# A two-layer attention and mixture-of-experts kernel: the products with the swapped rows of the rotation go from GpSimd to VectorE, from the fourth step on

## The chip, the cores and the metric

One core of one Trainium2 chip. The metric is the device time of one execution in microseconds (us). Names of engines in the rows: PE is TensorE's matmul, PEld its weight load, DVE is VectorE, ACT is ScalarE, POOL is GpSimd, SP is SyncE.

## The reference, cut to what matters

The input is 16 sequences of 256 tokens with 128 features. Two layers follow one another, each of them an attention and a feed-forward part that read the same normalised input and are added to it:

```python
xn = _layernorm(x)
x = x + L0_attn(xn) + L0_ffn(xn)      # windowed attention, 8 heads of 64; 8 experts of width 256 and a shared one
xn = _layernorm(x)
x = x + L1_attn(xn) + L1_ffn(xn)      # gated attention; 32 experts of width 64 and a shared one
```

The change touches the rotation of queries and keys in the attention of layer 0. The same projection `qk` serves as query and as key, with two tables each:

```python
bq = bq * jnp.cos(qf) * qs    + _rotate_half(bq) * jnp.sin(qf) * qs
bk = bk * jnp.cos(freqs) * inv_s + _rotate_half(bk) * jnp.sin(freqs) * inv_s
```

So for each of q and k there are two products (the rows with the cosine table, the swapped rows with the signed sine table) and one sum.

## The kernel before, in words

**Tiling and steps.** A step handles 2 sequences, 512 tokens; there are 8 steps, numbered 0 to 7. Features lie on the 128 partitions, tokens along the row, so most operands are tiles of 128x512 in float32. The 8 heads of layer 0 are handled as 4 pairs `p` (a pair fills 128 partitions), the 9 experts of layer 0 as `e` = 8 (the shared one) and 0 to 7.

**Stages.**
**The experts of layer 0.** For each expert TensorE makes two halves of the hidden layer (`up0_half`, lines 449 to 451), ScalarE applies Gelu (L1033), then the weight of the expert for each token is multiplied in: the half `c` = 0 on VectorE (`hidden`, L1405), the half `c` = 1 on GpSimd (`hidden`, L1773), both from the tile `pw` and the weights `wb` in SBUF. TensorE sums the results (`down0`, L586), for the half `c` only after that engine's event:

```python
w.wait_ge(*(HID_POOL if c else HID_DVE).at(s, e))
```

TensorE's order in `experts0` is: shared expert down; then `up0(1)`, `down0(0)`, `project(n, 0)`, `up0(2)`, `down0(1)`, `project(n, 1)`, `up0(3)`, `down0(2)`, `project(n, 2)`, `up0(4)`, `down0(3)`, `project(n, 3)`, `values(n, 0)`, `up0(5)`, `down0(4)`, `values(n, 1)`, `values(n, 2)`, `up0(6)`, `down0(5)`, `values(n, 3)`, `up0(7)`, `down0(6)`, `attention_out` (L594), `down0(7)`, with n = s + 1.

**PSUM banks.** `project(n, 0)` and `project(n, 2)` write bank 2, `project(n, 1)` and `project(n, 3)` bank 6 (L473); `values(n, 1)` writes bank 2 after `project(n, 2)` (L480). A bank that held a projection is free again at the event `STRAIGHT` of that pair, which the second product from PSUM counts up:

```python
freed[k] = STRAIGHT.at(s, p)
```

**The rotation of a pair**, before the change. `rope_in` on VectorE swaps neighbouring rows (`stream_shuffle`, L1324, PSUM to `qks`), multiplies the projection in PSUM by the two cosine tables (L1325 to `rtmp`, L1326 to `qka`, whose end is `STRAIGHT`). `rope_turn` on GpSimd multiplies the swapped rows by the two sine tables (L1759 to `kr`, L1761 to `qr`; both operands in SBUF). `rope_add` on VectorE adds (L1333, L1335; both operands in SBUF). The buffers `qks`, `rtmp` and `qka` have two slots, so `rope_in` of pair p waits for `rope_add` of pair p - 2. VectorE's order in `experts0` is `hidden` 0, 1, 2, `rope_in` 0, `hidden` 3, `rope_in` 1, `hidden` 4, `rope_add` 0, `rope_in` 2, `hidden` 5, `rope_add` 1, `rope_in` 3, `hidden` 6, `rope_add` 2, `hidden` 7, `rope_add` 3. GpSimd's is `hidden` 0, 1, `normalise` 0, 1 (L1767, the attention's division, once the denominators have come by DMA), `hidden` 2, `rope_turn` 0, `hidden` 3, `rope_turn` 1, `hidden` 4, `normalise` 2, 3, `hidden` 5, `rope_turn` 2, `hidden` 6, `rope_turn` 3, `hidden` 7.

Of the kernel before, what the change touches and what calls it, by code (L numbers as in the profile page):

```python
# [10 lines left out]
ALU = mybir.AluOpType  # L11
# [74 lines left out]
def two_layers(nc, A, out):  # L86
    pe, act, dve, pool, sp = nc.tensor, nc.scalar, nc.vector, nc.gpsimd, nc.sync
    with ExitStack() as ctx:
        def sb(name, shape, dt=F32):
            return ctx.enter_context(nc.sbuf_tensor(name, shape, dt))  # L90
# [4 lines left out]
        def event(name, per_step=1, unit=1):  # L95
            return Event(semaphore(name), per_step, unit)
# [4 lines left out]
        def weight(name, shape, src=None, dt=F32):  # L101
            t = sb("w_" + name, shape, dt)
            weights[name] = (t, A[name] if src is None else src)
            return t
# [5 lines left out]
        rope0 = weight("rope0", [P, 4, SEQ])  # L110
# [54 lines left out]
        qks = sb("qks", [P, 2, TOK])  # L165
        rtmp = sb("rtmp", [P, 2, TOK])
        qr = sb("qr", [P, PAIRS, TOK])
        kr = sb("kr", [P, PAIRS, TOK])
# [58 lines left out]
        def bank(k):  # L227
            return ps[:, k, :]
# [8 lines left out]
        def columns(s):  # L237
# [20 lines left out]
        PROJECTED, SWAPPED, STRAIGHT, TURNED_K, TURNED_Q, ROPED = (event(n, PAIRS) for n in (  # L258
            "projected", "swapped", "straight", "turned_k", "turned_q", "roped"))
        VALUES, VALUE_ROWS = event("values", TILES), event("value_rows", TILES)  # L260
        SCORES, MAXIMA, EXPS, INVERTED, WEIGHED, OUT_COLS = (event(n, UNITS) for n in (
            "scores", "maxima", "exps", "inverted", "weighed", "out_cols"))
# [36 lines left out]
        def spread(ap, dims):  # L299
            return bass.AP(tensor=ap.tensor, offset=ap.offset, ap=[list(ap.ap[0])] + [list(d) for d in dims])  # L300

        def seqs(ap):
            return ap.rearrange("p (g t) -> p g t", g=G)

        def table(rope, i):
            return spread(rope[:, i, :], [(0, G), (1, SEQ)])
# [968 lines left out]
        def dve_program():  # L1275
            w = Waits(dve)
# [42 lines left out]
            def rope_in(s, p, k):  # L1319
                h = p % 2  # L1320
                w.wait_ge(LOADED["rope0"], 16)
                w.wait_ge(*PROJECTED.at(s, p))
                w.wait_ge(*(ROPED.at(s, p - 2) if p >= 2 else KV1.at(s - 2)))
                dve.stream_shuffle(qks[:, h, :], bank(k), PAIR_SWAP).then_inc(*SWAPPED.one)  # L1324
                dve.tensor_tensor(seqs(rtmp[:, h, :]), seqs(bank(k)), table(rope0, 0), ALU.mult)  # L1325
                dve.tensor_tensor(seqs(qka[:, h, :]), seqs(bank(k)), table(rope0, 2),  # L1326
                                  ALU.mult).then_inc(*STRAIGHT.one)

            def rope_add(s, p):
                h = p % 2  # L1330
                w.wait_ge(*STRAIGHT.at(s, p))
                w.wait_ge(*TURNED_K.at(s, p))
                dve.tensor_tensor(kr[:, p, :], kr[:, p, :], rtmp[:, h, :], ALU.add)  # L1333
                w.wait_ge(*TURNED_Q.at(s, p))
                dve.tensor_tensor(qr[:, p, :], qr[:, p, :], qka[:, h, :], ALU.add).then_inc(*ROPED.one)  # L1335
# [193 lines left out]
            def attention(s):  # L1529
                first, second = s == 0, s == 1  # L1530
                if first:
                    maxima(s, 0)
                    maxima(s, 1)
                    rope_add(s, 1)
                    rope_in(s, 3, 1)
# [47 lines left out]
            def experts0(s):  # L1583
# [4 lines left out]
                if more:  # L1588
                    rope_in(n, 0, 2)
                hidden(s, 3)  # L1590
                if more:
                    rope_in(n, 1, 6)
# [136 lines left out]
        def pool_program():  # L1729
            w = Waits(pool)  # L1730
# [23 lines left out]
            def rope_turn(s, p):  # L1754
                h = p % 2
                w.wait_ge(LOADED["rope0"], 16)
                w.wait_ge(*SWAPPED.at(s, p))
                w.wait_ge(*SCORES.at(s - 1))
                pool.tensor_tensor(seqs(kr[:, p, :]), seqs(qks[:, h, :]), table(rope0, 1),  # L1759
                                   ALU.mult).then_inc(*TURNED_K.one)  # L1760
                pool.tensor_tensor(seqs(qr[:, p, :]), seqs(qks[:, h, :]), table(rope0, 3),  # L1761
                                   ALU.mult).then_inc(*TURNED_Q.one)

            def normalise(s, p):
                w.wait_ge(*DEN_WIDE.at(s))
                w.wait_ge(*OUT_COLS.at(s))
                pool.tensor_tensor(atc[:, p, :], atc[:, p, :], wide[:, p, :], ALU.mult).then_inc(*NORMALISED.one)  # L1767

            def hidden(s, e):
                n = 2 * place0(e) + 1  # L1770
                w.wait_ge(*GELU.at(s, n))
                w.wait_ge(*wb_layer0(e // 2, s))
                pool.tensor_tensor(hid[:, n % 4, :], hid[:, n % 4, :], wb[:, e, :],  # L1773
                                   ALU.mult).then_inc(*HID_POOL.one)
# [61 lines left out]
            def experts0(s):  # L1836
                n, more = s + 1, s < LAST
                for e in range(E0):
                    hidden(s, e)
                    if more and e in (2, 3, 5, 6):  # L1840
                        rope_turn(n, (0, 0, 0, 1, 0, 2, 3)[e])
                    if e in (1, 4):
                        normalise(s, 2 * (e // 4))
                        normalise(s, 2 * (e // 4) + 1)
# [44 lines left out]
            for s in range(STEPS):  # L1889
                attention(s)  # L1890
                if s == 1:
                    experts0_and_chain1(s)
                else:
                    experts0(s)
                if s:
                    experts1(s)
# [5 lines left out]
        act_program()  # L1902
        pool_program()
        dve_program()
        pe_program()

# [98 lines left out]
```

## Time and profile before

| what | value |
|---|---|
| three runs, median (lowest to highest) | 1113.2 us (1112.49 to 1113.9) |
| profiled execution: its own time | 1117.62 us |
| profiled execution: span from first to last instruction | 1116.3 us |
| mean granted clock of TensorE | 0.978 of full |
| PE busy | 1033.4 us (93%) |
| DVE busy | 713.6 us (64%) |
| ACT busy | 517.7 us (46%) |
| POOL busy | 472.3 us (42%) |
| time of one of the steps 3 to 6 | 131.5 us |

How to read it: a busy share is an average over stages that have different limits. The step's time is the distance between the starts of the same instruction in neighbouring steps, 467.11 us in step 3 and 598.58 us in step 4 for the down products of expert 3 (L586).

### The profile page before, as it was taken

How to read it: one execution, taken by the hardware profiler on the slowest of the kernel's cores; microseconds unless marked ns; L12 is line 12 of the kernel's file. 1: busy time of each engine (PE TensorE's matmuls, PEld its weight loads, DVE VectorE, ACT ScalarE, POOL GpSimd, SP SyncE). 2: the span in 40 equal slices, each digit the busy share in tenths (PEclk: the TensorE clock that was granted, in tenths of full speed). 3: DMA queues.
4: the chain of work that ended last, by engine and by line, in shares of the span. 5: the costliest groups of instructions: out<-in, count | busy, mean ns of one | idle time of the engine just before them, and what ended most of it. 6: DMA issues, size and time to landing. Idle time of an engine off the chain costs nothing.

```text
span 1116.3 us, 13293 instructions
## 1 busy us (share of the span) xinstructions
PE 1033.4 (93%) x4472; PEld 627.5 (56%) x4472; DVE 713.6 (64%) x1469; ACT 517.7 (46%) x1208; POOL 472.3 (42%) x353
## 2 busy tenths in 40 slices
PE   4799886899999989999899998999989998989988
PEld 2454554366555666556565565546655565655655
DVE  4658765748748487575857488484884758622833
ACT  3453672162554536444374525636265453634222
POOL 4747334434137521664208441285314741053433
PEclk9899997799999999999999999999999999989999
DMA  6040140060042302322023210422004120242051
GB/s 248 30 133 1 30 114 1 0 144 20 11 136 57 85 0 86 80 66 57 10 89 86 66 39 10 129 62 76 12 24 137 51 67 1 87 97 72 24 125 47
DMA packets 34581, 72.77 MB, mean 65 GB/s; under 512 B 4553, under 2 KB 5330, under 8 KB 34130
## 3 DMA queue, kind: packets, MB, share of 16 engines
q1 hardware_dynamic: 33074, 68.59, 22.1%
q10 hardware_dynamic: 1440, 3.35, 0.8%
q8 instruction: 35, 0.57, 0.2%
q14 instruction: 32, 0.26, 0.1%
HBM read 69.04 MB, written 2.88 MB: 64 GB/s over the span
## 4 chain that ended last, share of the span: by engine, by line
PE 70%; DVE 10%; issue 3%; POOL 3%; ACT 2%; DVEq 0%; POOLq 0%; ACTq 0%
PE ps L586 9%; PE ps L698 9%; PE ps L449 7%; PE ps L450 7%; PE ps L451 7%; PE ps L521 5%; PE ps L497 4%; PE ps L509 4%; PE ps L673 3%; PE ps L594 2%; PE ps L473 2%; PE ps L480 2%; PE ps L644 2%; PE ps L662 1%; PE ps L652 1%
## 5 line engine op out<-in xcount | busy, mean ns | idle before, releaser
L1773 POOL TENSOR_TENSOR pw<-pw,wb 128x512 f32<-128x512 f32 x64 | 94.1, 1471 | 204.9 <-ACT pw L1033 204.9
L1111 ACT ACTIVATE wide<-ps 128x512 f32<-128x512 f32 x136 | 81.0, 596 | 177.2 <-PE ps L451 176.4
L586 PE MATMUL ps<-pw,w_w 128*128 128x512 f32 x288 | 147.0, 627 | 16.9 <-DVE pw L1405 10.8
L1780 POOL TENSOR_TENSOR atc<-atc,wide 128x512 f32<-128x512 f32 x64 | 82.4, 1288 | 169.4 <-DVE atc L1520 169.4
L1033 ACT ACTIVATE pw<-ps,w_cols 128x512 f32<-128x512 f32 x144 | 98.5, 687 | 86.5 <-PE ps L451 83.5
L1405 DVE TENSOR_TENSOR pw<-pw,wb 128x512 f32<-128x512 f32 x64 | 61.8, 966 | 100.7 <-ACT pw L1033 100.6
L992 ACT ACTIVATE pw<-ps,nmax 128x256 f32<-128x256 f32 x256 | 117.3, 475 | 6.8 <-DVE nmax L1341 6.7
L1350 DVE COPY pt<-ps 128x512 f32<-128x512 f32 x128 | 82.3, 685 | 30.8 <-PE ps L509 30.8
L1341 DVE TENSOR_REDUCE nmax<-ps 128x4 f32<-128x1024 f32 x64 | 78.2, 1223 | 36.3 <-PE ps L497 35.8
L586 PEld LDWEIGHTS ps<-pw,w_w 128*128 128x128 f32 x288 | 52.9, 195 | 71.8 <-issue 26.2
L1780 POOL TENSOR_TENSOR pt<-pt,wide 128x512 f32<-128x512 f32 x48 | 61.5, 1281 | 67.3 <-DVE pt L1520 66.2
L449 PE MATMUL ps<-y1c,eg 128*128 128x512 f32 x112 | 84.8, 757 | 0.0
L449 PE MATMUL ps<-y0c,w 128*128 128x512 f32 x144 | 80.2, 557 | 1.2 <-ACT pt L1087 1.2
L521 PE MATMUL ps<-pt,vr 128*64 128x256 f32 x512 | 71.4, 401 | 8.0 <-DVE pt L1350 7.8
L1520 DVE TENSOR_TENSOR pt<-ps,wb 128x512 f32<-128x512 f32 x64 | 44.2, 691 | 49.0 <-PE ps L451 47.6
L509 PE MATMUL ps<-ident,pw 128*128 128x128 f32 x512 | 70.1, 280 | 5.8 <-ACT pw L992 3.6
L698 PE MATMUL ps<-pt,w_ed 128*128 128x512 f32 x128 | 66.6, 604 | 9.5 <-DVE pt L1524 9.5
L497 PE MATMUL ps<-kr,qr 64*128 64x256 f32 x512 | 74.5, 410 | 0.4 <-DVE qr L1335 0.4
L1520 DVE TENSOR_TENSOR atc<-ps,wb 128x512 f32<-128x512 f32 x64 | 44.1, 691 | 46.1 <-PE ps L451 39.5
L509 PEld LDWEIGHTS ps<-ident,pw 128*128 128x128 f32 x512 | 56.3, 142 | 25.2 <-issue 18.2
L698 PE MATMUL ps<-atc,w_ed 128*128 128x512 f32 x128 | 67.4, 608 | 0.0
L1751 POOL TENSOR_TENSOR rstd<-ve,half_power 128x8 f32<-128x8 f32 x16 | 28.5, 1783 | 88.2 <-DVE ve L1291 88.2
(223 smaller groups left out, 2188.2 us busy)
## 6 DMA issues: line engine op xcount, KB each, us to landing
wb<-scratch SPq DMA_DIRECT2D x128, 256.0 KB, 4.0
wb<-scratch SPq DMA_DIRECT2D x32, 512.0 KB, 5.7
wide<-scratch SPq DMA_DIRECT2D x16, 512.0 KB, 6.0
xin<-in_x SPq DMA_DIRECT2D x8, 256.0 KB, 2.9
out<-wide SPq DMA_DIRECT2D x8, 256.0 KB, 2.1
w_w<-in_w ACTq DMA_DIRECT2D x1, 1152.0 KB, 11.4
wb<-in_w SPq DMA_DIRECT2D x1, 1152.0 KB, 11.6
w_ed<-in_ed ACTq DMA_DIRECT2D x1, 1024.0 KB, 17.1
```

The source lines that it names most:

```text
L449: pe.matmul(bank(k), high, moving[:, 0, :], start=True, stop=False)
L497: m = pe.matmul(ps[:, b + par, qt * SEQ:(qt + 1) * SEQ], qr[rows, p, q0:q0 + P], kr[rows, p, g * SEQ:(g + 1) * SEQ], start=False, stop=Tru ...
L509: m = pe.transpose(bank(6 + par)[:, j * P:(j + 1) * P], pw[:, u % 2, 2 * par + qt, kt * P:(kt + 1) * P], ident[:, :])
L521: m = pe.matmul(bank(b)[64 * par:64 * par + 64, 0:SEQ], vr[:, 2 * g + kt, 2 * p + par, :], pt[:, u % 2, 4 * par + 2 * kt:4 * par + 2 * kt ...
L586: pe.matmul(bank(ACC), w2[:, e, c, :], hid[:, n % 4, :], start=n == 0, stop=n == 2 * E0 + 1).then_inc(*DOWN0.one)
L698: pe.matmul(bank(ACC), sd[:, :] if c < 0 else ed[:, c, :], hh[(c + 1) % len(hh)], start=c < 0, stop=c == CH1 - 1).then_inc(*DOWN.one)
L992: m = act.activation(pw[:, u % 2, j, :], ps[:, b + j // 2, (j % 2) * SEQ:(j % 2 + 1) * SEQ], ACT.Exp, bias=nmax[:, u % 3, j:j + 1], scale= ...
L1033: act.activation(hid[:, n % 4, :], bank(UPS[n % 4]), ACT.Gelu, bias=cols[:, C_B1 + 2 * e + c:C_B1 + 2 * e + c + 1], scale=1.0).then_inc(*G ...
L1350: dve.tensor_copy(pt[:, u % 2, 4 * par:4 * par + 4, :].rearrange("p a q -> p (a q)"), bank(6 + par)).then_inc(*PT.one)
L1520: dve.tensor_tensor(hh[h], bank(k), wb[:, c % (2 * RING), :], ALU.mult).then_inc(*HH_WEIGHED.one)
L1773: pool.tensor_tensor(hid[:, n % 4, :], hid[:, n % 4, :], wb[:, e, :], ALU.mult).then_inc(*HID_POOL.one)
L1780: pool.tensor_tensor(hh[h], hh[h], sgl[:, (c + 1) % 3, :], ALU.mult).then_inc(*HH_POOL.one)
```

## The change

From the fourth step on (step 3; it is prepared during step 2), `rope_in` on VectorE also makes the two products with the swapped rows, right behind its two products from PSUM, and GpSimd's program leaves `rope_turn` out. Steps 0, 1 and 2 are rotated as before: GpSimd's `rope_turn` for step 1 is in `experts0(0)`, for step 2 in `experts0_and_chain1(1)`. What is computed is the same.

```diff
--- before.py
+++ after.py
@@ -1325,6 +1325,13 @@
                 dve.tensor_tensor(seqs(rtmp[:, h, :]), seqs(bank(k)), table(rope0, 0), ALU.mult)
                 dve.tensor_tensor(seqs(qka[:, h, :]), seqs(bank(k)), table(rope0, 2),
                                   ALU.mult).then_inc(*STRAIGHT.one)
+                if s > 2:
+                    w.wait_ge(*SWAPPED.at(s, p))
+                    w.wait_ge(*SCORES.at(s - 1))
+                    dve.tensor_tensor(seqs(kr[:, p, :]), seqs(qks[:, h, :]), table(rope0, 1),
+                                      ALU.mult).then_inc(*TURNED_K.one)
+                    dve.tensor_tensor(seqs(qr[:, p, :]), seqs(qks[:, h, :]), table(rope0, 3),
+                                      ALU.mult).then_inc(*TURNED_Q.one)
 
             def rope_add(s, p):
                 h = p % 2
@@ -1837,7 +1844,7 @@
                 n, more = s + 1, s < LAST
                 for e in range(E0):
                     hidden(s, e)
-                    if more and e in (2, 3, 5, 6):
+                    if s < 2 and e in (2, 3, 5, 6):
                         rope_turn(n, (0, 0, 0, 1, 0, 2, 3)[e])
                     if e in (1, 4):
                         normalise(s, 2 * (e // 4))
```

On VectorE, in the middle of `experts0` of a step from 2 to 6, from the product of expert 3 on; first as it was (L1405 is `hidden`, L1324 to L1326 `rope_in`, L1333 and L1335 `rope_add`):

```order
L1405 TENSOR_TENSOR pw<-pw,wb 128x512
L1324 STREAM_SHUFFLE qks<-ps 128x512
L1325 TENSOR_TENSOR rtmp<-ps,w_rope 128x512
L1326 TENSOR_TENSOR qka<-ps,w_rope 128x512
L1405 TENSOR_TENSOR pw<-pw,wb 128x512
L1333 TENSOR_TENSOR kr<-kr,rtmp 128x512
L1335 TENSOR_TENSOR qr<-qr,qka 128x512
L1324 STREAM_SHUFFLE qks<-ps 128x512
L1325 TENSOR_TENSOR rtmp<-ps,w_rope 128x512
L1326 TENSOR_TENSOR qka<-ps,w_rope 128x512
```

The same place in the changed program, where `hidden` is L1412, the new products are L1331 and L1333, and the sums L1340 and L1342:

```order
L1412 TENSOR_TENSOR pw<-pw,wb 128x512
L1324 STREAM_SHUFFLE qks<-ps 128x512
L1325 TENSOR_TENSOR rtmp<-ps,w_rope 128x512
L1326 TENSOR_TENSOR qka<-ps,w_rope 128x512
L1331 TENSOR_TENSOR kr<-qks,w_rope 128x512
L1333 TENSOR_TENSOR qr<-qks,w_rope 128x512
L1412 TENSOR_TENSOR pw<-pw,wb 128x512
L1340 TENSOR_TENSOR kr<-kr,rtmp 128x512
L1342 TENSOR_TENSOR qr<-qr,qka 128x512
L1324 STREAM_SHUFFLE qks<-ps 128x512
L1325 TENSOR_TENSOR rtmp<-ps,w_rope 128x512
L1326 TENSOR_TENSOR qka<-ps,w_rope 128x512
```

The last row of both is the instruction that frees bank 2 for `values(n, 1)`. Between it and the projection of pair 0 there are four more instructions than before (those of pairs 0 and 1).

On GpSimd, in the same stage, as it was (L1773 is `hidden`, L1759 and L1761 `rope_turn`, L1767 `normalise`):

```order
L1773 TENSOR_TENSOR pw<-pw,wb 128x512
L1759 TENSOR_TENSOR kr<-qks,w_rope 128x512
L1761 TENSOR_TENSOR qr<-qks,w_rope 128x512
L1773 TENSOR_TENSOR pw<-pw,wb 128x512
L1759 TENSOR_TENSOR kr<-qks,w_rope 128x512
L1761 TENSOR_TENSOR qr<-qks,w_rope 128x512
L1773 TENSOR_TENSOR pw<-pw,wb 128x512
L1767 TENSOR_TENSOR atc<-atc,wide 128x512 x2
```

The whole of GpSimd's stage in the changed program, where `hidden` is L1780 and `normalise` L1774:

```order
L1780 TENSOR_TENSOR pw<-pw,wb 128x512 x2
L1774 TENSOR_TENSOR atc<-atc,wide 128x512 x2
L1780 TENSOR_TENSOR pw<-pw,wb 128x512 x3
L1774 TENSOR_TENSOR atc<-atc,wide 128x512 x2
L1780 TENSOR_TENSOR pw<-pw,wb 128x512 x3
```

Eight of its twenty instructions are gone, and nothing is left between the products of experts 2, 3 and 4. TensorE's and ScalarE's instructions are the same and in the same order.

## Rows read from the trace of the kernel before

**Rows 1.** The profile page: busy time of three engines, and the granted clock in slices.
```profile
PE 1033.4 (93%) x4472; PEld 627.5 (56%) x4472; DVE 713.6 (64%) x1469; ACT 517.7 (46%) x1208; POOL 472.3 (42%) x353
...
PEclk9899997799999999999999999999999999989999
```

**Rows 2.** Chain of waits, window 445 to 496 us: start, length, engine, output, line.
```profile
467.11 1.78 PE ps L586 x4
...
472.03 1.90 PE ps L586 x4
473.93 1.77 PE ps L480 x4
...
481.07 0.94 PE ps L586 x2
...
482.01 1.13 PE ps L586 x2
```

**Rows 3.** VectorE in order of time, window 440 to 500 us.
```profile
459.85 0.73 DVE L1324 STREAM_SHUFFLE qks<-ps 128x512 f32<-128x512 f32 x1
...
463.20 0.88 DVE L1405 TENSOR_TENSOR pw<-pw,wb 128x512 f32<-128x512 f32 x1 [1.45 <-ACT pw L1033]
...
467.17 1.08 DVE L1405 TENSOR_TENSOR pw<-pw,wb 128x512 f32<-128x512 f32 x1 [1.25 <-ACT pw L1033]
468.18 1.75 DVE L1333 TENSOR_TENSOR kr<-kr,rtmp 128x512 f32<-128x512 f32 x1
469.85 1.76 DVE L1335 TENSOR_TENSOR qr<-qr,qka 128x512 f32<-128x512 f32 x1
...
472.97 0.69 DVE L1326 TENSOR_TENSOR qka<-ps,w_rope 128x512 f32<-128x512 f32 x1
...
484.11 1.75 DVE L1405 TENSOR_TENSOR pw<-pw,wb 128x512 f32<-128x512 f32 x1
...
487.46 0.68 DVE L1335 TENSOR_TENSOR qr<-qr,qka 128x512 f32<-128x512 f32 x1
492.21 0.69 DVE L1515 TENSOR_TENSOR atc<-ps,wide 128x512 f32<-128x512 f32 x1 [4.08 <-ACT wide L1111]
```

**Rows 4.** GpSimd in order of time, same window.
```profile
459.69 2.62 POOL L1767 TENSOR_TENSOR atc<-atc,wide 128x512 f32<-128x512 f32 x2 [2.41 <-DMA wide<-scratch]
462.26 1.28 POOL L1773 TENSOR_TENSOR pw<-pw,wb 128x512 f32<-128x512 f32 x1
...
465.19 1.28 POOL L1761 TENSOR_TENSOR qr<-qks,w_rope 128x512 f32<-128x512 f32 x1
...
471.03 1.73 POOL L1773 TENSOR_TENSOR pw<-pw,wb 128x512 f32<-128x512 f32 x1
472.72 2.94 POOL L1767 TENSOR_TENSOR atc<-atc,wide 128x512 f32<-128x512 f32 x2
...
480.24 1.72 POOL L1773 TENSOR_TENSOR pw<-pw,wb 128x512 f32<-128x512 f32 x1
```

**Rows 5.** Waits by engine and line, window 445 to 490 us: total, times, longest.
```profile
PEld ps L480 <- DVE qka L1326: 0.6, 1, 0.6
```

**Rows 6.** Windows, step 7: length, busy PE, PEld, DVE, ACT, POOL, PEclk, DMA, GB/s.
```profile
985.40:988.80 3.40, 1.07 (x3) 0.20 (x2) 1.36 (x1) 0.92 (x2) 3.40 (x3) 1.00 0.61 145
988.80:992.20 3.40, 2.77 (x5) 1.55 (x6) 0.00 (x0) 0.00 (x0) 1.80 (x2) 0.50 0.08 20
992.20:995.60 3.40, 3.40 (x8) 1.98 (x7) 0.69 (x1) 1.37 (x2) 0.74 (x1) 0.50 0.56 146
```

**Rows 7.** The same view: inside step 0, and the end of step 3.
```profile
115.00:118.40 3.40, 0.99 (x7) 0.76 (x8) 3.19 (x10) 1.92 (x10) 0.00 (x0) 1.00 0.00 0
118.40:121.80 3.40, 3.40 (x17) 1.91 (x17) 2.72 (x12) 0.00 (x0) 2.12 (x2) 0.50 0.24 77
121.80:125.20 3.40, 3.40 (x30) 2.27 (x28) 2.96 (x6) 2.21 (x9) 3.18 (x4) 1.00 0.21 61
545.00:548.40 3.40, 1.99 (x7) 0.94 (x6) 3.16 (x7) 2.90 (x7) 0.00 (x0) 1.00 0.00 0
```

## The prediction

> **What bounds the kernel now.** The page comes first. TensorE is busy for 93% of the span, and its granted clock stands at 9 tenths or more through all of the middle [rows 1]. So time is won or lost where TensorE is made to stop, and the question for this change is whether VectorE or GpSimd makes it stop in the stage `experts0` of steps 2 to 6, where rotations for steps 3 to 7 are made. Steps 3 to 6 repeat to 0.1 us, so I read step 3 for all five.
>
> The chain of waits through that stage is TensorE from one end to the other [rows 2]. Its small stops can be read there: four matmul passes of `down0` in a row take 1.72 us when nothing is late (two take 0.86), so `down0(3)` with 1.78 has lost 0.06, `down0(4)` with 1.90 has lost 0.18, and `down0(6)`, 0.94 and 1.13 with 0.01 between, has lost 0.36 us. Together 0.6 us a step. The last, at 482.01, is GpSimd's product of expert 6, which ran from 480.24 to 481.96 [rows 4]: that half is late because a pair's sine products stand ahead of it on GpSimd.
>
> VectorE in order of time [rows 3] is the view that decides. Up to 467 it has gaps, 1.45 us ahead of `hidden` 3 and 1.25 ahead of `hidden` 4. From 467.17 to 488.1 it has none. The instruction that frees bank 2, L1326 of pair 2, starts at 472.97 and ends at 473.66; TensorE begins the values that need this bank at 473.93 [rows 2], and its weight load had waited for just that instruction [rows 5]. The margin there is 0.27 us.
>
> **What two engines do to each other.** A VectorE product of two SBUF tiles takes 0.68 us at 487.46, when GpSimd is idle, and 1.75 us at 468.18, when GpSimd works [rows 3]. A GpSimd product takes 1.28 us at 462.26 and 1.73 us at 471.03 [rows 4]. Instructions that read PSUM and one SBUF tile are not slowed: L1326 takes 0.69 us while GpSimd runs [rows 3, 4]. So where both want SBUF pairs they alternate: the VectorE product is held 1.07 us, the GpSimd product 0.45 us. Of the 0.68 us, 0.07 overlap with the next instruction (468.18 plus 1.75 against 469.85), so from start to start it is 0.61 free and 1.68 held. The Trainium skill, in "SBUF — State Buffer", section "Who interferes with whom", has the rule: the interface that both share is locked, and the second to come is blocked until the first has finished its whole instruction. That GpSimd's side waits only 0.45 us behind a product of 0.68 us is less than this rule gives; at the rule's 0.68 each alternation below would be about 0.23 us longer, seven of them 1.6 us a step, and the time about 8 us above my sum. The rows decide, so 0.45 stands.
>
> **The change, part by part.** It removes 8 of GpSimd's 20 products per step from 2 to 6 (40 in all) and adds 8 of two SBUF tiles to VectorE (40 in all), with no DMA and no other move. The waits added on VectorE (`SWAPPED`, `SCORES`) are for events long past: the shuffle is two instructions back. I take them at nothing; if they cost 0.1 us each, that is up to 0.4 us a step ahead of the bank.
>
> Free of any hold the 8 products are 8 x 0.61 = 4.9 us. Four of them, 2.4 us, lie ahead of the instruction that frees bank 2, and the two gaps of 2.7 us could just take them. What decides is the holding. The gaps were also the times at which VectorE stood out of GpSimd's way. I lay out VectorE after the shuffle of pair 0, which starts at 459.85 as before:
> - shuffle and two products from PSUM, 1.85 us, to 461.7.
> - first sine product: GpSimd is in its second `normalise` until 462.3 (459.69 plus 2.62 [rows 4]), held 0.5, to 462.8.
> - second sine product: held by GpSimd's `hidden` 2, 1.68, to 464.5.
> - `hidden` 3, ready since 463.2 [rows 3], held by GpSimd's `hidden` 3, 1.68, to 466.2.
> - pair 1: 1.85 to 468.0, then a free sine product (GpSimd waits for Gelu) to 468.6, then one held by `hidden` 4 to 470.3.
> - `hidden` 4, held by `normalise` 2, to 472.0; the first sum of pair 0, held by `normalise` 3, to 473.7; the second, held by `hidden` 5, to 475.4.
> - pair 2: a short wait for the sum, 0.1, then 1.85 us: bank 2 is free at 477.3.
>
> That is 5.6 us from PSUM, 8 products at 0.61, and 6.9 us held, where before it was 5.6, 4 products, 2.7 idle and 2.7 held. TensorE starts the values at 477.35 in place of 473.93, 3.4 us late. A weight load that could not be made ahead costs 0.27 more, as the 1.13 in place of 0.86 at 482.01 shows [rows 2]. That is 3.7 us a step. `hidden` 3 and 4 also end within 0.3 us of when TensorE asks, but that lateness lies inside the wait for bank 2.
>
> Behind it GpSimd has run dry and VectorE works unheld: the rest of pair 2, `hidden` 5, two sums, pair 3 and `hidden` 6 end near 484.7, just when TensorE comes (481.07 plus 3.7). So of the 0.36 us at `down0(6)` 0.27 stay. The last sum ends at 488.9, and VectorE's next work comes only at 492.21 plus the delay, behind 4.08 us of idle time [rows 3], so nothing of the delay is won back, and nothing is added. GpSimd gains 8 x 1.28 us or more of idle time for which nobody waits.
>
> **The clock.** A stop of 3.3 us has a second price. In step 7 TensorE was busy for 1.07 of 3.40 us, and then its clock was at half, the 1.2 GHz level, for 6.8 us [rows 6]; in step 0, 0.99 of 3.40 was followed by 3.4 us at half and then full clock [rows 7]; 1.99 busy of 3.40 at the end of step 3 left it at full [rows 7]. My stop is nearer the first two. Half clock for 3.4 us of work costs 1.7 us, less the 0.27 at `hidden` 6, which is then in time: 1.4 us a step. With 6.8 us at half, part of it inside the stop, it is about 2.6. I take the shorter one, since TensorE has work without a break behind this stop, as in step 0, while in step 7 it was interrupted again.
>
> **The sum:** 3.7 + 1.4 = 5.1 us a step, five steps, 25.5 us. The profiled execution took 1117.62 us, 4.4 above the median of 1113.2; against the median the forecast is 1138.7 us. Bounds of the unknown: no holding at all would give back the 0.6 us of small stops, 3.0 us faster; the clock at half twice as long in each step, 31.5 us slower.
>
> **The rivals.**
> - **Faster, 1110.2 us.** GpSimd with 12 products in place of 20 is out of the way, VectorE's sine products slip into the gaps, and the 0.6 us of stops per step go. For it: the free time of the new products, 2.4 us, fits into 2.7 us of gaps, and GpSimd's expert 6 is no longer late. It holds as long as bank 2 is free by 473.9, which leaves 14.05 - 5.6 - 4.9 = 3.5 us for holding. Against it: I count 6.9 us, seven meetings, and only three may happen. Chance 0.06.
> - **No change or little**, between 1111 and 1120 us, if about half the meetings happen. 0.06, of it 0.04 within 0.2%.
> - **The stop without the clock**: 5 x 3.7 = 18.5, 1131.7 us. For it: where the stop falls in time is open, and TensorE works right before and after. 0.20.
> - **The clock at half for 6.8 us each time**: 5 x 6.3 = 31.5, 1144.7 us. For it, rows 6. 0.23.
> - The forecast itself: 0.45. That the change doesn't do what it says is ruled out by the order of the instructions.
>
> **How the numbers follow.** The range takes in the three slower cases but for the edges: 1125 to 1149 us, the upper end with 0.5 us more a step if the added waits or a longer hold cost something. About 0.15 lies outside. A measurement of this kernel tells 0.2%, about 2.2 us, from no change. Faster by more 0.06, within 0.04, slower 0.90.
>
> **What would show it.** In the changed profile: L1331 and L1333 with a mean near 1.2 us, most of them 0.68 or 1.75; VectorE without a gap from 459.9 to bank 2; a wait of PE's L480 for DVE's L1326 of about 3.3 us, five times; GpSimd idle ahead of `hidden` 6; PEclk low right behind that wait. The forecast is wrong if L480 is not late, if TensorE's first late instruction is a `down0` that waits for `hidden`, or if the clock stays full in all five.

## The result, and the profile after

The changed kernel takes 1134.19 us (median of 4 runs, 1132.8 to 1136.67) against 1113.55 us of the kernel before beside it (4 runs, 1112.49 to 1115.12). The ratio is 1.0187 with an interval of 1.0163 to 1.021: slower by 20.6 us. The forecast was 1138.7 us, 25.5 us slower, in a range of 1125 to 1149.

Busy time and granted clock on the page of the changed kernel, which answer to [rows 1]:

```profile
PE 1035.6 (91%) x4472; PEld 629.2 (55%) x4472; DVE 732.4 (65%) x1509; ACT 517.2 (46%) x1208; POOL 414.8 (37%) x313
...
PEclk9799899899999999999999999999999999999999
```

TensorE's busy time and clock are nearly those of before. The span is 19.1 us longer (1135.4 against 1116.3) and TensorE is busy for 2.2 us more, so most of the added time, about 17 us, lies in stops of TensorE and not in its work.

**Where it lies.** ScalarE loads its table for Gelu at the start of the stage (L1033) and its table for SiLU at the end (L1111), so the distance of the two loads is the length of the stage `experts0` in which the rotation is made. In order of time on ScalarE in step 3, before:

```profile
445.17 1.28 ACT L1033 ACT_TABLE_LOAD   x1
...
490.19 1.28 ACT L1111 ACT_TABLE_LOAD   x1
```

and after:

```profile
447.58 1.28 ACT L1033 ACT_TABLE_LOAD   x1
...
497.57 1.28 ACT L1111 ACT_TABLE_LOAD   x1
```

That is 45.0 us before and 50.0 us after. In steps 2, 3, 4, 5 and 6 the same distance is 49.98, 49.99, 49.97, 49.98 and 48.58 us after the change, and 44.99 to 45.02 before: 23.4 us in all. Between these stages nothing grew: steps 2 to 5 have 86.4 us outside the stage in both profiles, step 6 has 86.0. Elsewhere the changed kernel's profiled execution was the shorter one: by 2.6 us ahead of step 2 (granted clock 0.95 there against 0.94, TensorE busy for 1.7 us less), and by 1.6 us in the stage of step 7 (42.40 us at a clock of 0.92 before, 40.82 us at 0.96 after). 23.4 - 2.6 - 1.6 is 19.2 us, the difference of the spans to 0.1 us.

**The stop.** Waits of TensorE over the whole execution, total, times and longest:

```profile
PE ps L480 <- DVE qka L1326: 17.0, 5, 3.4
```

This is the values' matmul waiting for the instruction that frees bank 2, five times 3.4 us. VectorE in order of time, step 3 (everything is 2.41 us later than before, as the two table loads of L1033 show):

```profile
462.27 0.73 DVE L1324 STREAM_SHUFFLE qks<-ps 128x512 f32<-128x512 f32 x1
...
464.10 1.18 DVE L1331 TENSOR_TENSOR kr<-qks,w_rope 128x512 f32<-128x512 f32 x1
465.20 1.76 DVE L1333 TENSOR_TENSOR qr<-qks,w_rope 128x512 f32<-128x512 f32 x1
466.88 1.75 DVE L1412 TENSOR_TENSOR pw<-pw,wb 128x512 f32<-128x512 f32 x1
...
470.38 0.68 DVE L1331 TENSOR_TENSOR kr<-qks,w_rope 128x512 f32<-128x512 f32 x1
470.98 1.75 DVE L1333 TENSOR_TENSOR qr<-qks,w_rope 128x512 f32<-128x512 f32 x1
...
474.34 1.76 DVE L1340 TENSOR_TENSOR kr<-kr,rtmp 128x512 f32<-128x512 f32 x1
476.02 1.75 DVE L1342 TENSOR_TENSOR qr<-qr,qka 128x512 f32<-128x512 f32 x1
...
479.12 0.68 DVE L1326 TENSOR_TENSOR qka<-ps,w_rope 128x512 f32<-128x512 f32 x1
...
485.95 1.75 DVE L1412 TENSOR_TENSOR pw<-pw,wb 128x512 f32<-128x512 f32 x1
...
499.59 0.69 DVE L1522 TENSOR_TENSOR atc<-ps,wide 128x512 f32<-128x512 f32 x1 [7.76 <-ACT wide L1111]
```

GpSimd beside it:

```profile
461.80 2.93 POOL L1774 TENSOR_TENSOR atc<-atc,wide 128x512 f32<-128x512 f32 x2 [2.11 <-DMA wide<-scratch]
464.68 3.39 POOL L1780 TENSOR_TENSOR pw<-pw,wb 128x512 f32<-128x512 f32 x2
470.65 1.53 POOL L1780 TENSOR_TENSOR pw<-pw,wb 128x512 f32<-128x512 f32 x1 [2.57 <-ACT pw L1033]
472.14 3.41 POOL L1774 TENSOR_TENSOR atc<-atc,wide 128x512 f32<-128x512 f32 x2
475.51 1.71 POOL L1780 TENSOR_TENSOR pw<-pw,wb 128x512 f32<-128x512 f32 x1
485.65 1.51 POOL L1780 TENSOR_TENSOR pw<-pw,wb 128x512 f32<-128x512 f32 x1 [8.43 <-ACT pw L1033]
```

The reader is to see three things. First, from 462.27 on VectorE has no gap but 0.1 us ahead of the shuffle of pair 2; the two that stood in [rows 3] are filled. Second, of the eight two-tile products up to the sum at 476.02, six take 1.75 or 1.76 us, the first 1.18, and one, at 470.38, is free with 0.68. Third, GpSimd's rows lie exactly beside the held ones: the second of its divisions from 461.80 holds the first product, its two `hidden` from 464.68 the next two, `hidden` at 470.65 one, the two divisions from 472.14 two, and `hidden` at 475.51 the last. Then GpSimd is idle until 485.65; VectorE is held again at 485.95. Bank 2 is free at 479.80, on the clock of before 477.4, where it was 473.7.

The end of the delay is in the same view: 7.76 us of idle time on VectorE ahead of L1522 in place of 4.08 [rows 3].

All 20 of the second sine products of a pair (shortest, median, longest in ns):

```profile
L1333 DVE TENSOR_TENSOR qr<-qks,w_rope x20: 678/1218/1757, 328.8 to 895.0; 128x512 f32<-128x512 f32 x20
```

**The clock.** Windows of step 3 around the stop (length, busy PE, PEld, DVE, ACT, POOL, granted clock), and then the same of step 6:

```profile
477.70:481.10 3.40, 1.25 (x3) 0.73 (x4) 3.28 (x8) 0.09 (x1) 0.00 (x0) 0.97 0.00 0
481.10:484.50 3.40, 3.40 (x8) 1.99 (x7) 3.28 (x7) 1.66 (x3) 0.00 (x0) 0.53 0.43 112
```

```profile
883.90:887.30 3.40, 1.76 (x4) 0.45 (x3) 3.28 (x4) 0.69 (x2) 2.52 (x2) 1.00 0.00 0
887.30:890.70 3.40, 1.65 (x5) 0.87 (x5) 3.40 (x6) 0.49 (x1) 0.00 (x0) 1.00 0.00 0
```

In step 3 the clock was at half, the 1.2 GHz level, for 3.4 us from about 481 on, a good 1 us after TensorE had begun again; so it was in steps 2, 4 and 5. In step 6 the same stop of 3.4 us had no low stretch at all: the clock stayed at full through it and behind it. That is the difference between 49.98 and 48.58 us: the low stretch costs 1.4 us, and without it the change costs 3.56 us a step. Why step 6 escaped the rows don't show. The busy times in the two pairs of lines differ only because the lines are laid differently over the stop: a line from 886.90 to 890.30, which lies over the stop of step 6 as the first lies over that of step 3, has the same 1.25 us busy, at full clock. The Trainium skill, "TensorE: Matmul & The Clock Gate", section "Why this matters for your kernels", warns of idle gaps between bursts of matmuls as what brings the clock down; four of the five stops agree, and the fifth, as long as they, does not.

### The profile page after: what moved, and what is told of

It reads as the page before. It is cut to its first block, busy times and chain, and to the rows that moved or that the text cites. A ratio compares the mean times of both kernels' runs of the same rounds, so it can differ in the third digit from the quotient of the medians.

```text
span 1135.4 us, 13288 instructions
## 1 busy us (share of the span) xinstructions
PE 1035.6 (91%) x4472; PEld 629.2 (55%) x4472; DVE 732.4 (65%) x1509; ACT 517.2 (46%) x1208; POOL 414.8 (37%) x313
## 4 chain that ended last, share of the span: by engine, by line
PE 61%; DVE 16%; issue 4%; POOL 3%; ACT 3%; DVEq 0%; POOLq 0%; ACTq 0%
PE ps L698 9%; PE ps L449 6%; PE ps L450 6%; PE ps L451 6%; PE ps L586 5%; PE ps L521 5%; PE ps L497 4%; PE ps L509 4%; PE ps L673 2%; PE ps L594 2%; DVE pw L1412 2%; PE ps L644 2%; PE ps L480 2%; DVE qr L1333 1%; PE ps L652 1%
## 5 line engine op out<-in xcount | busy, mean ns | idle before, releaser
L1780 POOL TENSOR_TENSOR pw<-pw,wb 128x512 f32<-128x512 f32 x64 | 95.2, 1492 | 265.4 <-ACT pw L1033 265.4
L1111 ACT ACTIVATE wide<-ps 128x512 f32<-128x512 f32 x136 | 80.9, 595 | 177.1 <-PE ps L451 176.3
L586 PE MATMUL ps<-pw,w_w 128*128 128x512 f32 x288 | 144.5, 620 | 16.9 <-DVE pw L1412 10.9
L1033 ACT ACTIVATE pw<-ps,w_cols 128x512 f32<-128x512 f32 x144 | 98.4, 687 | 87.4 <-PE ps L451 84.9
L1412 DVE TENSOR_TENSOR pw<-pw,wb 128x512 f32<-128x512 f32 x64 | 66.1, 1033 | 86.2 <-ACT pw L1033 86.2
L449 PE MATMUL ps<-y0c,w 128*128 128x512 f32 x144 | 83.1, 577 | 1.2 <-ACT pt L1087 1.2
```

Of the source, the lines that this page charges most:

```text
L449: pe.matmul(bank(k), high, moving[:, 0, :], start=True, stop=False)
L586: pe.matmul(bank(ACC), w2[:, e, c, :], hid[:, n % 4, :], start=n == 0, stop=n == 2 * E0 + 1).then_inc(*DOWN0.one)
L1033: act.activation(hid[:, n % 4, :], bank(UPS[n % 4]), ACT.Gelu, bias=cols[:, C_B1 + 2 * e + c:C_B1 + 2 * e + c + 1], scale=1.0).then_inc(*G ...
L1412: dve.tensor_tensor(hid[:, n % 4, :], hid[:, n % 4, :], wb[:, e, :], ALU.mult).then_inc(*HID_DVE.one)
```

## The experiments

Theory H, from the prediction: the delay comes of the places where VectorE's two-tile products meet GpSimd's, and of what stands ahead of the release of bank 2. Theory W, its rival: VectorE has simply been given more work than the stage has room for. In the diffs `n` is the step prepared. Lengths of the stage are read as above, from ScalarE's two table loads; clock times of a run are brought to the clock of before by the table load of L1033 in step 3, at 445.17 us there. The medians of before beside these runs are 1114.07 us for the first four (18 runs) and 1113.58 us for the others (18 runs).

### GpSimd's divisions later, VectorE untouched

```diff
-                    if e in (1, 4):
+                    if 1 < s < LAST and e == 5:
+                        for p in range(PAIRS):
+                            normalise(s, p)
+                    if not 1 < s < LAST and e in (1, 4):
                         normalise(s, 2 * (e // 4))
                         normalise(s, 2 * (e // 4) + 1)
```

> The changed kernel with VectorE untouched; in steps 2 to 6 GpSimd makes its four divisions (normalise) after the product of expert 5 in place of two after expert 1 and two after expert 4. Theory H (the delay is made of holding: VectorE's two-tile products meet GpSimd's): bank 2 is free at about 472.2 on the clock of the kernel before, 5 us earlier than in the change, so the wait of TensorE's L480 for VectorE's L1326 (3.4 us, five times) is gone. The meetings come later instead, around expert 6, whose product on VectorE ends near 484.7: a stop of about 3.7 us in front of down0(6) takes its place. Time about as the change, 1131 to 1145 us, with another stop. Theory W (the delay is only VectorE's added work, 8 products more whatever GpSimd does): the wait of L480 stays at 3.4 us, five times, and nothing stops at down0(6).

Measured: 1139.16 us (2 runs), ratio 1.0219, 1.0182 to 1.0256. The wait of 3.4 us at L480 is gone from all steps. TensorE's wait in the stage of step 3 (total, times, longest), VectorE in order of time, and GpSimd:

```profile
PE ps L586 <- DVE pw L1412: 4.0, 1, 4.0
```

```profile
474.89 0.69 DVE L1326 TENSOR_TENSOR qka<-ps,w_rope 128x512 f32<-128x512 f32 x1
...
486.35 1.74 DVE L1412 TENSOR_TENSOR pw<-pw,wb 128x512 f32<-128x512 f32 x1
```

```profile
477.87 6.34 POOL L1774 TENSOR_TENSOR atc<-atc,wide 128x512 f32<-128x512 f32 x4
```

Bank 2 is free at 475.58, which is 472.2 on the clock of before (3.39 us less), as laid out. The four divisions from 477.87 on, which end at 484.21, now hold two sums and part of a sine product ahead of `hidden` 6; the next sine product and `hidden` 6 itself are held by GpSimd's products of experts 6 and 7, which had waited behind the divisions. `hidden` 6 ends at 488.09, 484.7 on that clock, and TensorE stops 4.0 us for it. GpSimd's own product of expert 6 has become late by this edit as well, but it ends about 2 us sooner. The stage takes 50.1 to 50.3 us. So the same VectorE program misses another deadline when GpSimd's program alone is changed. W expected the wait at L480 to stay: it falls.

### What the change gives: GpSimd relieved, and nothing else

```diff
-                    if more and e in (2, 3, 5, 6):
+                    if s < 2 and e in (2, 3, 5, 6):
                         rope_turn(n, (0, 0, 0, 1, 0, 2, 3)[e])
...
-                w.wait_ge(*TURNED_K.at(s, p))
+                if s < 3:
+                    w.wait_ge(*TURNED_K.at(s, p))
```

(and the same for `TURNED_Q`, on the kernel before)

> The kernel before, with the 40 products with the swapped rows left out on both engines from step 3 on (so queries and keys of steps 3 to 7 keep old values in place of these terms). It takes from the change only what it gives: GpSimd's relief. Theory H: hidden 3, 4 and 6 are no longer late, 0.5 to 0.6 us a step, 2.5 to 3 us in all: 1110 to 1111 us against 1113.5. Rival R (GpSimd's relief frees more than the small stops, since earlier events let DMAs and the next stage start earlier): 5 us or more, below 1108.5 us.

Measured: 1111.75 us (10 runs), ratio 0.9967, 0.9946 to 0.9987. The stage takes 44.38 to 44.41 us in all five steps, 0.6 us less than before. The chain of waits in it shows where, against 1.78, 1.90 and 0.94 plus 1.13 in [rows 2]:

```profile
465.82 1.72 PE ps L586 x4
...
470.65 1.72 PE ps L586 x4
...
479.49 1.72 PE ps L586 x4
```

`down0(3)`, `down0(4)` and `down0(6)` all take 1.72 us, the time of four passes when nothing is late. Over the five steps that is the 3.1 us of the rival "faster" (the medians differ by 2.3), and it is all that the relief is worth.

### The same number of products, but from PSUM

```diff
+                if s > 2:
+                    w.wait_ge(*SCORES.at(s - 1))
+                    dve.tensor_tensor(seqs(kr[:, p, :]), seqs(bank(k)), table(rope0, 1),
+                                      ALU.mult).then_inc(*TURNED_K.one)
+                    dve.tensor_tensor(seqs(qr[:, p, :]), seqs(bank(k)), table(rope0, 3),
+                                      ALU.mult).then_inc(*TURNED_Q.one)
                 dve.tensor_tensor(seqs(rtmp[:, h, :]), seqs(bank(k)), table(rope0, 0), ALU.mult)
                 dve.tensor_tensor(seqs(qka[:, h, :]), seqs(bank(k)), table(rope0, 2),
                                   ALU.mult).then_inc(*STRAIGHT.one)
-                if s > 2:
-                    w.wait_ge(*SWAPPED.at(s, p))
-                    w.wait_ge(*SCORES.at(s - 1))
-                    dve.tensor_tensor(seqs(kr[:, p, :]), seqs(qks[:, h, :]), table(rope0, 1),
-                                      ALU.mult).then_inc(*TURNED_K.one)
-                    dve.tensor_tensor(seqs(qr[:, p, :]), seqs(qks[:, h, :]), table(rope0, 3),
-                                      ALU.mult).then_inc(*TURNED_Q.one)
```

> The changed kernel with the 40 products on VectorE in the same number and nearly the same place, but reading the projection in PSUM in place of the swapped rows in SBUF (so the swapped rows are not what is multiplied), and put ahead of the two straight products, so that the bank is freed after them. One SBUF tile per product, so nothing to hold. Theory H: VectorE does all the added work (about 0.6 us each) and is still in time: bank 2 is free at about 473.4, no wait at L480, and 0.5 us a step faster than before, 1110 to 1112 us. Theory W: the added work is there in full and even ahead of the bank's release, so the wait at L480 stays above 2.4 us a step (four products of 0.6 us) and the time above 1125 us.

Measured: 1109.05 us (6 runs), ratio 0.9956, 0.9937 to 0.9975. The stage takes 44.4 to 44.5 us in four steps and 44.9 in one. VectorE and GpSimd in order of time:

```profile
457.00 0.68 DVE L1327 TENSOR_TENSOR kr<-ps,w_rope 128x512 f32<-128x512 f32 x1
457.59 0.68 DVE L1329 TENSOR_TENSOR qr<-ps,w_rope 128x512 f32<-128x512 f32 x1
...
461.18 0.67 DVE L1327 TENSOR_TENSOR kr<-ps,w_rope 128x512 f32<-128x512 f32 x1
...
469.25 0.68 DVE L1332 TENSOR_TENSOR qka<-ps,w_rope 128x512 f32<-128x512 f32 x1
469.85 1.26 DVE L1411 TENSOR_TENSOR pw<-pw,wb 128x512 f32<-128x512 f32 x1
```

```profile
455.95 2.88 POOL L1773 TENSOR_TENSOR atc<-atc,wide 128x512 f32<-128x512 f32 x2 [2.16 <-DMA wide<-scratch]
...
460.48 1.27 POOL L1779 TENSOR_TENSOR pw<-pw,wb 128x512 f32<-128x512 f32 x1 [0.42 <-ACT pw L1033]
```

The products at 457.00 and 457.59 run in the middle of GpSimd's two divisions and take 0.68 us; the one at 461.18 runs beside `hidden` and takes 0.67. In the change the two products of pair 0, at the same place beside the divisions and `hidden`, took 1.18 and 1.76 us. Bank 2 is free at 469.93, 473.4 on the clock of before (3.49 us more), although all added work stands ahead of its release. This is the run that tells the theories apart: VectorE has room for 40 more products, and what it has no room for is holding.

### Two of the four products behind the release of the bank

VectorE's order in steps 2 to 6, with H for `hidden`, R for `rope_in`, M for the two sine products, A for `rope_add`:

```diff
-H0 H1 H2 R0 M0 H3 R1 M1 H4 A0 R2 M2 H5 A1 R3 M3 H6 A2 H7 A3
+H0 H1 H2 R0 M0 H3 R1 H4 A0 R2 M1 M2 H5 A1 R3 M3 H6 A2 H7 A3
```

> The changed kernel with the two sine products of pair 1 moved on VectorE from behind that pair's straight products to behind those of pair 2, so that they no longer stand ahead of the release of bank 2. Nothing else is moved. Theory H, laid out as in the prediction: bank 2 is free at about 474.0, TensorE waits there 0.3 us in place of 3.4, and then hidden 5 and hidden 6 are each late by 0.3 to 1 us: in all 1.4 us a step over the kernel before and no fall of the clock in these steps, so about 7 us slower than before, near 1120 us. Theory W: two products fewer ahead of the bank save 1.2 of the 3.4 us, so 2.2 us of wait at L480 stay, and 2.5 us a step or more, over 1126 us with the clock's part.

Measured: 1119.3 us (7 runs), ratio 1.0057, 1.0037 to 1.0077, 5.2 us slower. The stage takes 46.3 us in steps 2, 3 and 5, 1.3 over before, 46.4 in step 6 and 47.1 in step 4. VectorE in order of time, and TensorE's wait in the stage:

```profile
472.73 0.68 DVE L1326 TENSOR_TENSOR qka<-ps,w_rope 128x512 f32<-128x512 f32 x1
...
481.05 0.68 DVE L1414 TENSOR_TENSOR pw<-pw,wb 128x512 f32<-128x512 f32 x1
```

```profile
PE ps L586 <- DVE pw L1414: 0.8, 1, 0.8
```

Bank 2 is free at 473.41, 474.0 on the clock of before: 3.4 us earlier than in the change, although only two products of 0.68 us were moved. With them went two held times of 1.07 us: that of the second of the two, and that of `hidden` 4, which no longer meets GpSimd. (The first of the two had been free.) L480 does not wait to speak of. What is late now is `hidden` 6 at 481.05, for which TensorE stops 0.8 us, and the clock stays at full. The size came out as laid out (1.3 us against 1.4); of its parts, `hidden` 5 was expected late too, and no wait for it shows.

### All of it on VectorE, in an order that avoids the meetings

```diff
-H0 H1 H2 R0 M0 H3 R1 M1 H4 A0 R2 M2 H5 A1 R3 M3 H6 A2 H7 A3
+H0 H1 H2 R0 R1 M0 H3 A0 H4 R2 M1 M2 H5 A1 A2 H6 R3 M3 A3 H7
```

> The changed kernel (all 8 sine products of a step on VectorE, reading the swapped rows in SBUF), with VectorE's order in steps 2 to 6 rewritten: sine products and sums are put where GpSimd is between two of its products, and hidden 6 ahead of pair 3. Same instructions, same tiles. Theory H (the delay is a matter of where VectorE's two-tile products meet GpSimd's, and of what stands ahead of the bank): laid out by hand with 0.61 us free and 1.68 us held, TensorE never stops for VectorE or GpSimd in this stage; the stage, 45.0 us before and 50.0 in the change, is 44.4 us; five times 0.6 us faster than before, about 3 us. Theory W (VectorE simply has too much to do in this stage): some stop of TensorE for VectorE stays wherever it is put, the stage is over 46 us, the time over 1120 us.

Measured: 1109.62 us (10 runs), ratio 0.9964, 0.9951 to 0.9978. ScalarE's two table loads of step 3, and VectorE:

```profile
441.44 1.28 ACT L1033 ACT_TABLE_LOAD   x1
...
485.83 1.28 ACT L1111 ACT_TABLE_LOAD   x1
```

```profile
459.91 0.68 DVE L1333 TENSOR_TENSOR kr<-qks,w_rope 128x512 f32<-128x512 f32 x1
...
462.18 0.68 DVE L1414 TENSOR_TENSOR pw<-pw,wb 128x512 f32<-128x512 f32 x1
...
474.49 0.67 DVE L1414 TENSOR_TENSOR pw<-pw,wb 128x512 f32<-128x512 f32 x1
```

44.4 us, as in three other steps and 5.6 us less than in the change with the same instructions. Both straight parts come first, while GpSimd divides; of the products of pair 0 one is held, and then GpSimd waits for Gelu. `hidden` 6 starts at 474.49 with pair 3's work behind it, 478.2 on the clock of before. In step 4 the stage took 45.1 us; there GpSimd's divisions began 3.4 us after it was ready, waiting for the denominators' DMA, and `hidden` 2 stood behind them.

### The kernel before, in a better order

```diff
-VectorE H0 H1 H2 R0 H3 R1 H4 A0 R2 H5 A1 R3 H6 A2 H7 A3
+VectorE H0 H1 H2 R0 H3 R1 A0 H4 R2 H5 A1 H6 R3 H7 A2 A3
-GpSimd  H0 H1 N0 N1 H2 M0 H3 M1 H4 N2 N3 H5 M2 H6 M3 H7
+GpSimd  H0 H1 N0 H2 M0 H3 N1 H4 N2 M1 H5 N3 H6 M2 M3 H7
```

(N is a division, `normalise`)

> The kernel before (sine products on GpSimd), with both orders in steps 2 to 6 rewritten: GpSimd takes the product of the next expert ahead of divisions and sine products where it can, VectorE takes sums before hidden and hidden 6 and 7 earlier. If the 0.6 us a step of small stops are all that is to be had, this gives them as well as the change does in a good order: a stage of 44.4 us, about 3 us faster than before. If moving work to VectorE has a worth of its own, it falls behind g5_new_order by more than 0.2 us a step.

Measured: 1109.87 us (9 runs), ratio 0.9967, 0.9952 to 0.9981, with a stage of 44.4 us but in step 4 (45.2). This cannot be told from the run before it: where the sine products run is worth nothing by itself that these runs could tell. In the stages both orders only take back the 0.6 us a step, in step 4 nothing: 2.4 and 2.3 us in all, as in the run from PSUM (2.4). The medians are lower by 3.7 to 5.0 us in these three runs; the rest lies elsewhere, in the profiled executions in good part in the stage of step 7 (39.2 to 39.4 us against 42.40), whose instructions they leave as they were.

### The best version: the new order, and the divisions of step 7 later

```diff
-                    if e in (1, 4):
+                    if e in ((3, 4) if s == LAST else (1, 4)):
                         normalise(s, 2 * (e // 4))
```

> g5_new_order, and in step 7, where GpSimd's first two divisions wait for the denominators' DMA ahead of the products of experts 2 and 3 and TensorE stands still for 3.0 us, these divisions go behind the product of expert 3. The stop of 3.0 us goes, and the stretch at half clock behind it (3.4 or 6.8 us long, 1.7 to 3.4 us of work). So step 7's stage, 42.4 us before and 39.2 to 40.8 in the other runs, comes to about 36 to 37, and the time to 5 us or so below g5_new_order, near 1106 us. If GpSimd's division then makes the product of expert 4 late, 1 us of it stays.

Measured: 1105.41 us (4 runs), ratio 0.9928, 0.9901 to 0.9955; 8.2 us less than before, and 4.2 less than without the second part, whose range (1106.57 to 1112.21) lies above this one's (1104.72 to 1105.93). The stage of step 7 takes 36.76 us in place of 42.40, and of 39.39 in the profile of the run without the second part: there TensorE still stopped for 2.9 us, but the clock did not fall behind it. So 2.6 us are the stop itself, and the rest is a low stretch that this stop has in some executions. GpSimd in order of time, and windows of 10 us in that stage (length, busy PE, PEld, DVE, ACT, POOL, granted clock):

```profile
976.50 1.27 POOL L1795 TENSOR_TENSOR pw<-pw,wb 128x512 f32<-128x512 f32 x1 [1.83 <-ACT pw L1033]
...
980.85 2.97 POOL L1789 TENSOR_TENSOR atc<-atc,wide 128x512 f32<-128x512 f32 x2
```

```profile
975.00:985.00 10.00, 10.00 (x35) 6.18 (x34) 2.09 (x3) 4.76 (x7) 6.66 (x5) 1.00 0.64 147
985.00:995.00 10.00, 9.73 (x29) 5.08 (x28) 4.01 (x3) 3.49 (x6) 7.17 (x6) 1.00 0.20 52
```

The products of experts 2 and 3 no longer wait for the DMA, TensorE is busy for 10.00 and 9.73 of 10 us there, and the clock stays at full, where [rows 6] had a stop and 6.8 us at half.

## Why the prediction was right

- **What bounds the stage.** TensorE was the chain, and bank 2, with its margin of 0.27 us, was the deadline that broke. Right: five waits of L480 for L1326.
- **The laying out of VectorE.** It gave 1 partly held product, 6 fully held, 1 free, and the bank free at 477.3. Measured: 1.18 us, six of 1.75 or 1.76, one of 0.68, and 477.4. Each of GpSimd's products named there is the one that holds. The stop was forecast at 3.7 us a step with the weight load; step 6, without the clock's part, shows 3.56.
- **The second deadline.** `hidden` 3 and 4 were late by little and inside the wait, as said. `hidden` 6 was forecast unheld, ending at 484.7. In step 6 it was (896.28, which is 484.7 by that step's table load). In step 3 it was held after all (1.75 us at 485.95) and ended at 485.3 on the clock of before; it cost nothing, since TensorE, slowed by the low stretch, came for it 1.1 us later still.
- **Nothing won back.** Right: VectorE's idle time behind the stage grew from 4.08 to 7.76 us, and the next stages did not change.
- **The clock.** Forecast: 3.4 us at half and 1.4 us a step. Measured: just this in four steps, nothing in the fifth. So the piece of the sum that was off is that it charged all five: 4 x 4.97 + 3.56 = 23.4 us in place of 25.5. That one of five would escape was open; the rival "without the clock" had it for all. The reason given for the shorter stretch, work without a break behind the stop, was not tested, so its being right may be luck.
- **The rest of the difference,** 23.4 us in the stages against 20.6 us of the medians, is not settled by single executions. The profiled execution of the kernel before was 4.1 us above its median, that of the change 2.5 above. Step 7's stage shows how much can move by itself: its stop of 2.6 to 3.0 us is in all eight profiles that have it, and the stage takes 42.2 and 42.4 us (clock 0.92), 40.7 and 40.8 (0.96), or 39.15 to 39.4 (1.00). The prediction had no term for this.
- **A sign that was off.** L1331 and L1333 were both to have a mean near 1.2 us. L1333 has (1218 ns); L1331 has 827 ns, which is also what the prediction's own laying out gives, where only the first of a step's four is held in part.
- **The rivals.** "Faster" had the right size for its gain (3.0 us; the relief alone gave 0.6 us a step) but its condition, bank 2 free by 473.9, is not enough. The run from PSUM and the one in the new order meet it, and both are 0.4% faster than before; the run with the late divisions meets it too (472.2) and is the slowest of all, because `hidden` 6 is a second deadline. What the change lacked was the order.
- **The rule on the shared interface.** The chip's 1.75 us beside GpSimd and 0.68 without repeat in every run, and so does the 0.66 to 0.69 of products with one SBUF tile. By the rule's full hold the bank would, by the prediction's estimate, have been free 1.6 us later; it came to 0.1 us where the 0.45 us of the rows had put it.

## What to carry to other kernels

Before moving an engine's work, lay its instructions out in time beside those of the engine with which it shares a way to SBUF, with the held and the free duration of each; the meetings ahead of a deadline can weigh more than the added work (here they held VectorE 4.2 us longer than before, 6.9 against 2.7, with 2.4 us of work added). A gap on a busy engine may be what keeps it out of the other's way, so filling it costs more than the length of the work. And look first whether an order alone gives what the move is to bring: here it gave the same on either engine (3.7 and 4.0 us). An engine can have more than one deadline in a stage: here an order that met the first, bank 2, still missed the second, `hidden` 6.

## What the runs showed of the hardware

- Stops of TensorE of one length had different ends. Of five stops of 3.4 us with the same instructions around them, four were followed by 3.4 us at half clock and one by none; stops of 2.6 to 3.0 us in step 7 were followed by a mean clock of 0.92, 0.96 or 1.00 over the stage. One low stretch of 3.4 us is worth 1.4 us here. What decides whether it comes is not shown.
- A VectorE product of two SBUF tiles took 1.75 us where it met a GpSimd product and 0.68 where it met none; one with a PSUM source took 0.68 us in both places. Moving two products out of the way made the bank free 3.4 us earlier, 1.2 us for their own time and 2.1 us for two held times that went with them.
- In the changed kernel the steps 2 to 5 take 136.4 us each with a fall of the clock in every one; step 6, 134.6 us without. Before, these were 131.4 to 131.5 and 131.0 us.
